# Scaling the attention probabilities of three heads on ScalarE in place of VectorE, in seven of eight batches

## The reference

```python
q = (xn @ w_q.T).reshape(B, S, 16, 32).transpose(0, 2, 1, 3)   # 16 heads share one k and one v
k, v = jnp.split(xn @ w_kv.T, 2, axis=-1)
q, k = rotary(q * w, pos, xscale), rotary(k * w, pos, 1 / xscale)
attn = jnp.einsum('bnih,bjh->bnij', q, k)
attn = jnp.where(causal, -big, attn)
attn = jax.nn.softmax(attn, axis=-1)
out = jnp.einsum('bnij,bjd->bind', attn, v)
```

## Time and profile before

| | before |
|---|---|
| median of 3 runs | 1720.31 us (1719.22 to 1723.76) |
| the profiled execution | 1720.09 us |
| its span, first to last instruction | 1718.3 us |
| TensorE busy (matmuls) | 1616.7 us, 94% |
| VectorE busy | 1184.0 us, 69% |
| ScalarE busy | 1092.5 us, 64% |
| GpSimd busy | 825.9 us, 48% |
| mean granted TensorE clock | 0.987 of full speed |

### The profile page before, as it was taken

One profiled execution on the slowest core, in us unless ns is written; L12 is line 12 of the kernel. 1 busy time (PEld: TensorE's weight loads), 2 busy tenths in 40 slices (PEclk: granted clock), 3 DMA queues, 4 the chain that ended last, 5 costly groups with the idle time before them and its releaser, 6 DMA issues.

```text
span 1718.3 us, 40612 instructions
## 1 busy us (share of the span) xinstructions
PE 1616.7 (94%) x10811; PEld 1383.5 (81%) x10811; DVE 1184.0 (69%) x3611; ACT 1092.5 (64%) x2852; POOL 825.9 (48%) x673
## 2 busy tenths in 40 slices
PE   5787889999999999999999999899999999999999
PEld 4776667777787787787778777799999999999987
DVE  6779777867777778678687777355555555555567
ACT  3368765757757756667577567366666666666642
POOL 0213023435524534345244253377777877778760
PEclk9899899999999999999999999999999999999999
DMA  7954614434434444344343345499999999998794
GB/s 276 394 168 143 106 52 139 138 109 140 133 102 151 141 120 139 109 152 139 97 152 121 123 133 153 113 184 191 187 194 181 191 189 200 197 174 160 137 267 177
DMA packets 193090, 273.71 MB, mean 159 GB/s; under 512 B 37400, under 2 KB 133791, under 8 KB 190820
## 3 DMA queue, kind: packets, MB, share of 16 engines
q0 software_dynamic: 60352, 92.59, 25.1%
q1 hardware_dynamic: 77572, 113.01, 23.1%
q10 hardware_dynamic: 54944, 65.52, 12.8%
HBM read 121.83 MB, written 129.67 MB: 146 GB/s over the span
## 4 chain that ended last, share of the span: by engine, by line
PE 68%; DVE 16%; issue 7%; ACT 4%; DMA 4%; DVEq 1%; SPq 0%; ACTq 0%; POOL 0%; POOLq 0%
PE e_psH L1729 14%; PE e_psY L1740 14%; DVE m_sc L1108 5%; PE m_psO L1358 4%; PE e_psX L1714 4%; PE m_psU L64 3%; PE m_psT L1336 3%; PE m_psS L1311 3%; PE m_psU L66 3%; PE m_psU L65 3%; PE m_psY L64 3%; PE m_psY L65 3%; PE m_psY L66 3%; DVE m_sc L1120 2%; ACT m_sc L942 2%
## 5 line engine op out<-in xcount | busy, mean ns | idle before, releaser
L1694 POOL DMA_INDIRECT sums<-e_y,e_where x287 | 445.9, 1554 | 156.0 <-issue 91.5
L864 POOL DMA_INDIRECT slot_rows<-m_row,slots x256 | 267.0, 1043 | 461.5 <-ACT m_sc L942 428.9
L942 ACT ACTIVATE m_sc<-m_sc,m_low 128x512 f32<-128x512 f32 (+3 forms) x512 | 283.5, 556 | 126.4 <-DVE m_low L1108 124.7
L1729 PE MATMUL e_psH<-e_xt,e_w_of 128*128 128x128 f32 x2296 | 305.0, 276 | 3.3 <-ACT e_xt L1589 3.3
L1740 PE MATMUL e_psY<-e_w,e_ht 128*128 x1148 | 295.8, 380 | 1.3 <-ACT e_ht L1600 1.2
L1108 DVE CUSTOM_DVE_ANT_0 m_sc<-m_psS,cst 128x512 f32<-128x512 f32 (+3 forms) x512 | 229.8, 485 | 91.9 <-PE m_psS L1311 89.9
L1729 PEld LDWEIGHTS e_psH<-e_xt,e_w_of 128*128 128x128 f32 x2296 | 280.3, 192 | 3.7 <-ACT e_xt L1589 3.5
L1595 ACT ACTIVATE e_w_of<-e_w 128x512 f32 x287 | 180.9, 630 | 119.4 <-issue 115.5
L1740 PEld LDWEIGHTS e_psY<-e_w,e_ht 128*128 128x128 f32 x1148 | 196.4, 191 | 17.0 <-issue 2.1
L1311 PE MATMUL m_psS<-m_ks,m_qs 96*128 96x256 f32 (+2 forms) x512 | 158.6, 369 | 42.4 <-DVE m_low L1108 35.1
L1650 DVE TENSOR_SCALAR e_where<-e_row,e_shifts 128x1 uint32<-128x1 uint32 x287 | 61.4, 214 | 196.8 <-DMA sums<-e_y,e_where 178.4
(11 more groups left out here) (235 smaller groups left out, 3245.4 us busy)
## 6 DMA issues: line engine op xcount, KB each, us to landing
e_row<-slot_rows ACTq DMA_DIRECT2D x287, 144.5 KB, 3.4
m_qs<-m_qhi SPq DMA_DIRECT2D x256, 64.0 KB, 2.0
e_w<-in_w SPq DMA_DIRECT2D x256, 64.0 KB
f_xt<-in_x SPq DMA_DIRECT2D x8, 1024.0 KB, 11.5
m_qs<-m_qlo SPq DMA_DIRECT2D x128, 64.0 KB, 2.0
m_res<-in_x SPq DMA_DIRECT2D x8, 1024.0 KB, 6.4
sums<-empty POOLq DMA_DIRECT2D x32, 256.0 KB
partial<-m_res ACTq DMA_DIRECT2D x16, 512.0 KB
```

Of the source, the lines that this page charges most:

```text
L864: pool.indirect_dma_start(out=xs, out_offset=bass.IndirectOffsetOnAxis(ap=slots_sb[:, g, k:k + 1], axis=0), in_=row[g % 2][:, :], in_offse ...
L942: nc.scalar.activation(cols, cols, ACT.Exp, bias=low[:, h % 2, i:i + 1], scale=-1.0, accum_out=total[:, h % 2, i:i + 1]).then_inc(exp_done, 1)
L1694: pool.indirect_dma_start(out=both_sums, out_offset=bass.IndirectOffsetOnAxis(ap=where[u % NY][:, 0:1], axis=0), in_=y[u % NY][:, :], in_o ...
L1729: mm = pe.matmul(psH[u % 2][:, k * P:(k + 1) * P], w1_of[u % 2][:, c * INTER + k * P:c * INTER + (k + 1) * P], xt[u % 2][:, c * P:(c + 1) ...
```

## The change

From batch 1 on, the heads 1, 5 and 9 are scaled by ScalarE, in the place in its slot where batch 0 has it, after the last copy of the head before. VectorE still takes the reciprocal of these heads and then goes on. Batch 0 stays as it was.

```diff
-SCALED_BY_ACT = range(9)
+SCALED_BY_ACT = {True: range(9), False: (1, 5, 9)}
...
                     if 0 <= t < NH:
                         ta(t, 2)
-                    if first and s in SCALED_BY_ACT:
+                    if s in SCALED_BY_ACT[first]:
                         scale(s)
...
                     dve.wait_ge(inv_made, at(b, NH, h + 1))
-                    if first and h in SCALED_BY_ACT:
+                    if h in SCALED_BY_ACT[first]:
                         return
```

## The result

The changed kernel takes **1749.87 us** (median), beside 1719.76 us for the kernel before on the same chip: a recorded ratio of 1.0187, 95% interval 1.0155 to 1.0219; the two medians alone make 1.0175. Three of the four executions of the changed kernel took 1747.70 to 1751.57 us at a mean granted clock of 0.988 to 0.991; the fourth took 1766.48 us at 0.940, and no trace shows where its clock was lower. The forecast was 1749.0 us. The two profiled executions, 1748.16 and 1720.09 us, differ by 28.1 us where the sum gave 28.9.

What follows compares the result with a forecast made beforehand. TensorE work was taken as 68% of the span, with VectorE mattering only where TensorE waits for masking. Delays of 1.02 + 1.55 + 1.56 = 4.13 us a batch, times 7, added 28.9 to 1720.1: 1749.0 us, range 1739 to 1756.

Steps and rivals of the forecast that it cites:

- the sum: Delays after slots 1, 5 and 9: 1.02 + 1.55 + 1.56 = 4.13 us a batch, times 7 = 28.9 us.
- The links: Chain from ScalarE's scaling: exponentials, transposed copy, rounding, low part, next masking, TensorE; 1.02 to 1.56 us late; chance 0.79.
- ScalarE's cost: Four multiplies ahead of the next head's exponentials take 1.81 us of ScalarE, read from slot 5 of batch 0.
- Slot 5: Head 5's scaling makes transposes 1.40, reciprocal 1.24 and low part 1.55 us later, delaying the masking of head 7.
- the rival of the smaller loss: Rounding does not hold up the low part, only the reciprocals count: 22.3 us more, 1742 us; chance 0.10.
- Slots 1 and 9: Scaling heads 1 and 9 makes the low part behind it 1.02 and 1.56 us later.
- the bound: Slot 1: masking of head 2 could start at most 0.28 us earlier, limited by its scores on TensorE.
- VectorE's relief: Multiplies taken off VectorE gain nothing in slots 5 and 9, 0.28 us in slot 1; rival that VectorE bounds: chance 0.05.
- the rival put at 0.04: TensorE's clock falls after new waits in slots 5 and 9 of each batch: 33.6 us more, 1782.6 us; chance 0.04.
- the 2.4 us estimated as the most: Clock rival's highest cost per occurrence: a quarter of a 10 us stretch of batch 0 at granted clock 0.76.
- Does the delay reach the end?: Delays end in maskings TensorE waits for in slots 3, 7, 11 and carry through the batch; rival transfer swallowing them: 0.02.

Runs made afterwards that it cites:

- the idle multiplies: Kernel before, VectorE still scaling, plus four unread ScalarE multiplies at the end of slots 1, 5 and 9 in batches 1 to 7: 1765.9 us, ratio 1.0261.
- the early place: The change's heads 1, 5 and 9 scaled by ScalarE earlier in the slot, between first copy and shared expert's work: 1739.23 us, ratio 1.0107 to the kernel before.
- the bias rows: Kernel before with a batch's four bias rows all at the end of slot 8, not one in each of slots 5 to 8: 1714.42 us, ratio 0.9962.

## Why the prediction was right

The links that the forecast replayed came as forecast, one by one. That the median lies 0.9 us from the forecast is in part luck: the interval of the ratio leaves 26.7 to 37.7 us for the difference.

**ScalarE's cost.** 1.81 us from the first scaling to the exponential, taken from batch 0, is 427.14 - 425.33 = 1.81 us in batch 2.

**Slot 5, link by link.** From the masking of head 6 to each step, after against before: exponentials 2.71 and 0.89 (+1.82); transposes 2.87 and 1.46 (+1.41; forecast 1.40); reciprocal 5.03 and 3.78 (+1.25; forecast 1.24); low part 6.76 and 5.17 (+1.59; forecast 1.55); masking of head 7 7.97 and 6.38 (+1.59). That the low part waits 0.23 us for the rounding (L923) behind the reciprocal's own +1.25 is what set aside the rival of the smaller loss: the rounding does hold it up.

**Slots 1 and 9.** Slots 9 and 10 together grew by 1.59 us (forecast 1.56), slots 1 and 2 by 1.04 (forecast 1.02). In slot 1 the masking of head 2 came 0.31 us earlier (the bound was 0.28), and nothing of it survived slot 2, which grew by 1.35.

**VectorE's relief.** Forecast at nothing in slots 5 and 9, since VectorE waited 0.17 and 0.43 us for TensorE there, and at most 0.28 us in slot 1. The kernel with the scaling left out shows 0.01 us in slot 5, 0.00 in slot 9 and 0.27 in slot 1. This is where the Trainium skill's page Perfetto Trace Analysis, under Optimizing Scalar/DVE Operations, could have misled: it names offloading to ScalarE as a choice where VectorE is saturated. VectorE's busy share of 5.89 in 6.23 us looked like that case, but the change is 1.87% slower (the recorded ratio), and the kernel with the scaling left out puts the most that it could have given at 0.11%.

**The clock.** In the profiled execution the rival put at 0.04 did not come: slots 1, 5 and 9 ran at 1.00, and so did slots 6, 7 and 11. But its danger was nearer than the forecast knew. One of the four executions, 1766.48 us long, had a mean granted clock of 0.940; whether its lower clock came in these slots is not shown. And the forecast weighed the rival by waits of up to 1.4 us. Single waits of 1.5 to 2.8 us, which the idle multiplies made of the same delay, were followed by the lower clock in 16 of 21 slots, at 0.4 to 1.8 us a slot in place of the 2.4 us estimated as the most. The Trainium skill's page TensorE: Matmul & The Clock Gate (Part 1) has the lower clock as the default that activity lifts; the granted clock of 0.53 behind the 2.80 us wait agrees with that. Why it stayed at 1.00 behind one of 2.77 us, no run here shows.

**Does the delay reach the end?** The last masking of batch 7 and the experts' first matmul, by line (durations in ns, first and last start in us), before:

```profile
L1108 DVE CUSTOM_DVE_ANT_0 m_sc<-m_psS,cst x512: 280/485/694, 114.1 to 1061.4; 128x512 f32<-128x512 f32 x43, 128x128 f32<-128x128 f32 x43, 128x256 f32<-128x256 f32 x43, 128x384 f32<-128x384 f32 x42
...
L1729 PE MATMUL e_psH<-e_xt,e_w_of x2296: 272/275/422, 1089.6 to 1658.7; 128*128 128x128 f32 x192
```

and after:

```profile
L1108 DVE CUSTOM_DVE_ANT_0 m_sc<-m_psS,cst x512: 280/486/693, 114.1 to 1090.6; 128x512 f32<-128x512 f32 x43, 128x128 f32<-128x128 f32 x43, 128x256 f32<-128x256 f32 x43, 128x384 f32<-128x384 f32 x42
...
L1729 PE MATMUL e_psH<-e_xt,e_w_of x2296: 273/275/422, 1117.2 to 1686.7; 128*128 128x128 f32 x192
```

To the last masking the delay is 29.2 us, 4.17 a batch (forecast 4.13, 28.9 in all). By the experts' first matmul it is 27.6. The missing 1.6 us is none of the links: behind the last batch TensorE waits 3.28 us for VectorE in both kernels, and in the stretch after it the clock differs. Before, then after:

```profile
1070.00:1080.00 10.00, 7.18 (x24) 5.73 (x25) 3.19 (x5) 1.75 (x4) 0.00 (x0) 0.83 0.44 111
```

```profile
1099.20:1109.20 10.00, 7.16 (x31) 5.79 (x32) 3.88 (x6) 1.78 (x4) 0.00 (x0) 1.00 0.42 110
```

So the sum was 0.3 us too small up to there, and the total 0.8 us too large, because the kernel before lost time to the clock once where the changed one did not. That the lower clock made all of the 1.6 us is read from these two rows and was not tried by itself.

**Where expectations of the experiments failed.** For the idle multiplies a slot's loss was foreseen and the clock was not. For the early place the loss of batch 2 was put at 2.3 us and came to 2.52, most of the difference in slots 9 and 10, where the exponentials came 1.08 us late in place of 0.9. For the bias rows the gain was put at 0.9 us a batch and came to 1.17 in batch 2; over the execution it was 5.7 us between the medians, a little under the expected 6 to 8.

## What to carry to other kernels

Before work is moved off a busy engine, look at its next instruction on the path: if that one waits for someone else already (0.17 and 0.43 us here), the relief turns into waiting, whatever the busy share says. Then look at the receiving engine's idle time at that very place: 1.81 us of ScalarE cost 1.0 to 1.6 us ahead of the exponentials and nothing in a slot where ScalarE still waited for TensorE afterwards. And before the longest row of a table of waits is attacked, follow what is behind it: with the 24.9 us row removed, the same time stood in the next one.

## What was not expected of the hardware

How a delay is cut up went with its price. In the profiled execution of the change the 46 us of TensorE's waiting in batches 1 to 7 came as waits of at most 1.35 us, and the clock of those slots stayed at 1.00. With the idle multiplies the same 46 us came with two waits joined into one of 1.5 to 2.8 us; 16 of 21 such waits were followed by a granted clock of 0.52 to 0.74, and the median was 16 us longer (1765.9 against 1749.87). But the change is not safe from the lower clock either: one of its four executions took 1766.48 us at a mean of 0.940. Nor does the length of a wait alone decide: 1.46 us was followed by a granted clock of 0.72 and 2.77 us by 1.00, 2.19 us by 0.72 and 2.18 us by 1.00 (slot 11 of batches 2 and 3), and 3.28 us by 0.83 in one kernel and 1.00 in another. What else decides stays open.
